# One layer of cross-attention, self-attention and a routed FFN: later waits and another PSUM bank where cross-attention hands over to self-attention

## The reference

```python
x = x + xattn(layernorm(x), ctx, mask, Wq, Wk, Wv, Wo)   # 16 heads of 32, 64 x 512 scores a sequence
x = x + attn(layernorm(x), wq, wk, wv, wo)               # rotary positions, causal, 64 x 64 scores
x = x + ffn(layernorm(x), w_router, W1, b1, W2, b2)      # half of each sequence's tokens, 512 -> 2048 -> 512
```

```python
# self-attention, the stage that begins where the change is
q, k, v = x @ wq, x @ wk, x @ wv
q, k = rope(q), rope(k)
scores = where(causal, q @ k.T / sqrt(32), -inf)
x = x + (softmax(scores) @ v) @ wo
```

## Time and profile before

| what | value |
|---|---|
| time, median of three executions | 1379.94 us (1377.67 to 1382.29) |
| time of the profiled execution | 1377.36 us |
| its span, first to last instruction | 1374.9 us |
| TensorE busy | 1341.6 us, 98% of the span |
| ScalarE, VectorE, GpSimd busy | 730.2, 666.7, 544.3 us |
| mean granted clock of TensorE | 0.995 of full speed |

### The profile page before, as it was taken

The page is one execution under the profiler, slowest core; times in us unless marked ns, Lnnn a source line. Parts: engine busy times, 40 slices in busy tenths (PEclk is TensorE's granted clock), DMA queues, the critical chain, the costliest instruction groups (busy, mean ns, idle before and its releaser), DMA issues.

```text
span 1374.9 us, 33152 instructions
## 1 busy us (share of the span) xinstructions
PE 1341.6 (98%) x12984; PEld 1059.8 (77%) x12984; DVE 666.7 (48%) x1688; ACT 730.2 (53%) x1410; POOL 544.3 (40%) x284
## 2 busy tenths in 40 slices
PE   7999999999999999999999999999999998999998
PEld 6877777777777777777777777677888886878686
DVE  4254554554544544544544544455666567732323
ACT  6455655656656656656656656653333345453231
POOL 6442422422522422422432434724444444466342
PEclk9999999999999999999999999999999999999999
DMA  7021111011011010110120112010000002122241
GB/s 254 26 59 34 34 50 32 28 54 32 25 57 32 25 57 26 31 57 25 32 57 25 32 56 93 14 55 2 1 0 0 0 0 93 62 92 92 77 138 61
DMA packets 39324, 66.06 MB, mean 48 GB/s; under 512 B 4208, under 2 KB 8560, under 8 KB 39280
## 3 DMA queue, kind: packets, MB, share of 16 engines
q1 hardware_dynamic: 38848, 64.67, 14.7%
q10 hardware_dynamic: 432, 0.79, 0.2%
HBM read 61.25 MB, written 4.19 MB: 48 GB/s over the span
## 4 chain that ended last, share of the span: by engine, by line
PE 89%; DVE 2%; ACT 2%; issue 1%; POOL 1%; POOLq 0%; DVEq 0%; ACTq 0%
PE psum L204 39%; PE psum L957 9%; PE psum L252 8%; PE psum L1791 6%; PE psum L1762 6%; PE psum L222 5%; PE psum L240 5%; PE psum L261 3%; PE psum L972 3%; PE psum L990 1%; PE psum L1448 1%; PE psum L982 1%; PE psum L1000 1%; PE psum L1773 1%; PE psum L1019 0%
## 5 line engine op out<-in xcount | busy, mean ns | idle before, releaser
L300 ACT ACTIVATE PT<-psum 128x512 f32<-128x512 f32 x256 | 153.2, 598 | 228.4 <-PE psum L252 228.4
L287 ACT ACTIVATE prob<-prob,nmx 128x512 f32<-128x512 f32 x256 | 182.6, 714 | 94.4 <-DVE nmx L342 94.4
L356 DVE COPY V<-psum 128x512 f32<-128x512 f32 x128 | 88.5, 692 | 229.4 <-PE psum L204 229.4
L342 DVE CUSTOM_DVE_ANT_0 prob<-psum,mbias 128x512 f32<-128x512 f32 x256 | 165.4, 684 | 67.1 <-PE psum L222 67.1
L293 ACT ACTIVATE prob<-prob,rinv 128x512 f32<-128x512 f32 x256 | 182.7, 714 | 0.0
L489 POOL TENSOR_SCALAR ctx_a<-ctx_r 128x1536 fp32r<-128x1536 f32 x16 | 65.4, 4090 | 265.3 <-PE psum L204 265.1
L489 POOL TENSOR_SCALAR ctx_b<-ctx_r 128x1536 fp32r<-128x1536 f32 x16 | 65.4, 4090 | 252.3 <-PE psum L204 235.4
L252 PEld LDWEIGHTS psum<-ident,prob 128*128 128x128 f32 x1024 | 127.5, 141 | 34.4 <-issue 1.3
L252 PE MATMUL psum<-ident,prob 128*128 128x128 f32 x1024 | 153.2, 272 | 0.5 <-ACT PT L300 0.4
L204 PE MATMUL psum<-wv_h,ctx_b 128*128 128x512 f32 x384 | 144.4, 417 | 0.0
L204 PE MATMUL psum<-wv_h,ctx_a 128*128 128x512 f32 x384 | 142.2, 412 | 1.2 <-DVE K L356 1.2
(11 more groups left out here) (215 smaller groups left out, 2814.2 us busy)
## 6 DMA issues: line engine op xcount, KB each, us to landing
ctx_r<-in_ctx SPq DMA_DIRECT2D x32, 768.0 KB, 4.6
w_r<-in_L_ffn_W SPq DMA_DIRECT2D x64, 256.0 KB, 2.8
xres<-in_x SPq DMA_DIRECT2D x16, 256.0 KB, 2.6
out<-tok SPq DMA_DIRECT2D x13, 256.0 KB, 3.6
tok<-in_x SPq DMA_DIRECT2D x3, 1024.0 KB, 12.4
mask<-in_mask_BxS_bf SPq DMA_DIRECT2D x32, 64.0 KB, 4.1
tok<-in_x SPq DMA_DIRECT2D x4, 256.0 KB, 3.3
wq_r<-in_L_xattn_Wq SPq DMA_DIRECT2D x4, 256.0 KB, 5.0
```

The costliest lines, as they stand in the source:

```text
L287: act.activation(prob[:, r, :], prob[:, r, :], ACT.Exp, bias=nmx[:, r:r + 1], scale=-1.0, accum_out=rsum[:, r:r + 1]).then_inc(s_ex, 1)
L300: act.activation(PT[:, r, :, :].rearrange("p k n -> p (k n)"), T_bank, ACT.Copy).then_inc(s_Pt, 1)
L342: dve.tensor_tensor_reduce(prob[:, r, :], S_bank[r], mbias[:, b, :], 1.0, 3.0e38, ALU.add, ALU.min, nmx[:, r:r + 1]).then_inc(s_mx, 1)
L356: dve.tensor_copy(item_place(q, m), KV_bank[m % 2]).then_inc(s_KVe, 1)
```

## The change

Three edits, all at the passage from cross- to self-attention.

1. TensorE's wait for `s3_xl` (tokens of tile 0 split into high and low parts) moves out of `first_tokens`, from ahead of item 1 to behind it, ahead of the first `pe_turn`, which is the next instruction that writes `T_bank`.
2. The transposed tokens of tiles 2 and 3 (steps 0 and 1) go to bank 2, no longer to bank 3, and TensorE waits for the rotation of Q (`s3_rq`), no longer for that of K (`s3_rk`), before it writes them.
3. The subtraction for `ow_l` on VectorE in step 1 moves from ahead of the rotation of K to behind `x3_l` of tile 3, ahead of the row sums.

```diff
@@ pe_group
             if fill:
                 fill()
             pe_item(pe, g, q, 1)
+            if filled:
+                pe.wait_ge(*filled)
             pe_turn(pe, g, q, 0, first)
@@ pe_cross
             def first_tokens():
                 pe.wait_ge(s_Pt, SLOTS - 8)
                 pe_x(pe, 0, T_bank)
-                pe.wait_ge(s3_xl, 1)
...
+                    if last and q == GPT - 2:
+                        pe_group(pe, g, q, first, fill=first_tokens, filled=(s3_xl, 1))
@@
+        def x_bank(t):
+
+            return bank[2] if isinstance(t, int) and t < 4 else bank[3]
@@ pe3
             if has(t + 2):
-                pe.wait_ge(s3_rk, 2 * t + 4)
-                pe_x(pe, t + 2, bank[3])
+                if isinstance(t, int) and t < 2:
+                    pe.wait_ge(s3_rq, 2 * t + 4)
+                else:
+                    pe.wait_ge(s3_rk, 2 * t + 4)
+                pe_x(pe, t + 2, x_bank(t + 2))
@@ act3, dve3
-                act_x(act, t + 2, par, bank[3])
+                act_x(act, t + 2, par, x_bank(t + 2))
...
-                dve_x(dve, t + 2, par, bank[3])
+                dve_x(dve, t + 2, par, x_bank(t + 2))
@@ dve3
             if isinstance(t, int) and t == 1:
                 shifts(dve, slice(G - 2, G), 2)
-                dve.wait_ge(s3_wa, 1)
-                dve.tensor_tensor(ow_l[:], ow_r[:], ow_h[:].bitcast(F32), ALU.subtract).then_inc(s3_wd, 1)
...
+            if isinstance(t, int) and t == 1:
+                dve.wait_ge(s3_wa, 1)
+                dve.tensor_tensor(ow_l[:], ow_r[:], ow_h[:].bitcast(F32), ALU.subtract).then_inc(s3_wd, 1)
             if has(t):
                 dve.wait_ge(s3_ex, t + 1)
```

More of the change, by code:

```diff
@@ L263, in pe_outputs, with pe_group @@
             ins.then_inc(s_Wo, 1)
-        def pe_group(pe, g, q, first=False, fill=None):
+        def pe_group(pe, g, q, first=False, fill=None, filled=None):
             pe_scores(pe, g, q, first)
@@ L795, in first_tokens @@
                 pe_x(pe, 0, T_bank)
-                pe.wait_ge(s3_xl, 1)
             def tile(g, first, last):
                 for q in range(GPT - 1 if last else GPT):
-                    pe_group(pe, g, q, first, fill=first_tokens if last and q == GPT - 2 else None)
+                    if last and q == GPT - 2:
+                        pe_group(pe, g, q, first, fill=first_tokens, filled=(s3_xl, 1))
+                    else:
+                        pe_group(pe, g, q, first)
             pe_item(pe, 0, -1, 2)
```

## The result

The changed kernel takes 1373.53 us (median of 6 runs, 1372.96 to 1374.11), the kernel before in the same comparison 1378.93 us (median of 6, 1377.67 to 1382.29). The ratio is 0.996, with a 95% interval of 0.9949 to 0.997: 0.4% faster. A second comparison gave 1373.81 against 1378.27 us, a ratio of 0.9965 (0.9951 to 0.9978). The forecast of 1376.0 us lies above both. Its range of 1373.2 to 1379.4 holds them, the first with 0.3 us to spare. In both the gain is over 0.3%, to which I had given a chance of 0.42; "within 0.3%" had 0.54.

What follows compares the result with a forecast made beforehand. TensorE, busy 98% of the span, was taken to bound the kernel. From 1379.94 us, 3.0 us (2.1 + 0.9) for the order of work and 0.9 us for the clock came off: 1376.0 us, range 1373.2 to 1379.4.

Steps and rivals of the forecast that it cites:

- Edit 1, 2.1 us: At tile 0, TensorE does item 1 before waiting for `x_l`: 2.1 us gained, bounds 1.5 and 2.15.
- Edit 2, nothing: Ahead of the token transposes of tiles 2 and 3, gaps of 0.50 and 0.61 us go, but nothing is gained.
- Edit 3, 0.9 us and not 2.1: At tile 2, `q_r` gets 2.1 us shorter, but K's last matmul limits the gain to 0.9 us, bounds 0 and 0.9.
- Where `ow_l` goes: Ahead of the row sums, `ow_l` waits for GpSimd's subtraction; the scaling still ends in time, with 2.3 us of slack.
- The gap at V stays: Ahead of V of tile 2, TensorE still waits some 2.2 us for `o_l`, only shifted.
- Sum 3.0 us: Whole passage: 2.1 us from the wait behind item 1 plus 0.9 us from moving `ow_l` later.
- The clock's 0.9 us: Removing the 2.15 us gap before `x_l` of tile 0 saves a 1.85 us clock fall, one chance in two: 0.9 us.
- B, the clock stays up at V of tile 2: Rival: no clock fall behind the gap at V of tile 2, 1.85 us more gained, 1374.2 us; chance 0.20.
- A: The forecast as computed for the whole kernel: 1376.0 us, own range 1374.2 to 1378.0; chance 0.52.
- C: Rival at tile 2: `q_r` is long because it directly follows the scaling, so moving `ow_l` gives nothing: 1376.9 us; chance 0.13.
- Case D: Rival in the stage behind the passage: more or longer clock falls give back 3.7 us, 1379.7 us; chance 0.10.
- E: Rival, slower: clock falls at the FFN's short waits; two more cost 3.7 us, four 7.4 us (1384.3); chance 0.05.

Runs made afterwards that it cites:

- changed, again: The changed kernel with all three edits, measured a second time beside the kernel before: 1373.81 us, ratio 0.9965.
- cut alone: The changed kernel with the subtraction for `ow_l` cut in three and its banks unchanged: 1374.27 us, ratio 0.9964 to the kernel before.

## Why the prediction was right, and where not

*Edit 1, 2.1 us*: right. 2.10 in the changed kernel's profile, and the same distance in edit 1 alone.

*Edit 2, nothing*: right, as far as it can be measured. Alone 0.9999, and the changed kernel without it is as fast.

*Edit 3, 0.9 us and not 2.1*: right. 0.89 in the profile, with K's last matmul as the new last wait.

*Where `ow_l` goes*: right. VectorE waits for GpSimd's subtraction. The scaling was forecast for 939.38 to 941.29, which with the 2.10 of edit 1 and the 0.79 of the start is 936.49 to 938.40; it runs from 936.27 to 938.18. The transposes that wait for it come at 939.14 and find it done, with 1.0 us to spare, less than the 2.3 of the forecast because the clock stayed up. By the Trainium skill (SBUF — State Buffer, "Who interferes with whom") the one that starts first keeps the port for its instruction; the trace agrees, 3.12 for 2.28 us here. In the version with `ow_l` in three, the half of it starts at 924.54 and takes its 1.21 us, and `q_r`, at 924.56, takes 2.34 us.

*The gap at V stays*: right, 2.11 us.

*Sum 3.0 us*: right for the order of work (2.10 + 0.89).

*The baseline*: 1.0 of the 2.5 us between forecast and result is not the change's. The forecast was counted from 1379.94 us, the median of three executions, and the kernel before stood at 1378.93 beside the changed one. The gain forecast was 3.9 us, measured were 5.4 and 4.5 us.

*The clock's 0.9 us*: the term that was wrong in its reason. The step was "the first gap, with one chance in two". Edit 1 alone, which removes that gap, shows no higher mean clock (0.9946). The changed kernel does: 0.9965 against 0.9945, which is 2 x 0.0020 x 1376 = 5.5 us less time at half clock. At most half of that, 2.8 us, is time won, and it will be less, because some of that time costs nothing: in the profile before, the granted clock is 0.50 from 1372.0 us to the end at 1374.9, and TensorE has no instruction there.

A better estimate comes from how the executions of one and the same kernel differ. Over 182 executions of all the kernels (each compared with the mean of its own kernel in its own comparison) 0.001 of mean clock goes with 0.6 us of span, so 0.0020 goes with about 1.2 us, an estimate that could be 0.6 us off either way. The mean span fell by 4.8 us, from 1376.4 to 1371.6: 3.0 by the order of work, about 1.2 with the clock, and some 0.6 that no run explains. The 0.35 us outside the span come on top. So 0.9 us was near the size of the clock's part, but by luck, since it was put at a gap that does not bring it.

How the higher clock comes about is not settled. The gap at V lowered the clock in 7 of the 9 profiles that have it, but only in two of the four whose order of work there is the changed kernel's (yes in changed, again, and without edit 2; no in changed and cut alone), and in none of the five in which the gap is filled or gone. That makes shorter and fewer gaps in the passage a likely cause, but each edit alone moved the mean clock by 0.0009 at most, about as much as before moved between comparisons (0.9939 to 0.9949), and there is one profile of each kernel, two of the changed one.

*B, the clock stays up at V of tile 2*: this rival, with 0.20 and 1374.2 us, is nearer to both medians than A. Its condition held in the changed kernel's first profile and not in the second, and in the first the low stretch that it saved came back at 1149. So neither A nor B describes every execution.

*C* is refuted: `q_r` directly behind the scaling takes 1.27 us. *Case D*, a longer low stretch later, is what the first profile shows at 1149 (twice 3.4 us); it came beside the gain and did not cancel it. *E* did not come: no fall behind the short waits of the FFN in the changed kernel's two profiles; the profile without edit 2 has one at 1273.6 us, 10.2 us long.

Of the signs that would have shown the prediction wrong none came: the chain still goes through `o_l` in step 1, TensorE does not wait for the scaling in step 2, and there are two low stretches before TensorE ends, for three.

## What to carry to other kernels

Put a wait at the instruction that overwrites, not at the one that happens to come next, and before counting on the length of a gap look at the chain: of three edits the one that removed two visible gaps gave nothing, since TensorE only waited for the next link. When an instruction that slowed a neighbour is moved away, the gain ends at the next last wait, here 0.9 of 2.1 us. The next edit is then the wait that TensorE still shows (`o_l`): another bank for what it guards, together with `ow_l` cut into idle times of VectorE so that the scaling is in time, gave 1.7 us more by the order of work and 3.7 in the median. Look at what the moved work meets at its new place.

## What the runs showed of the hardware that I had not expected

TensorE can stand without anything it waits for in the profile while a burst of DMAs lands, here eight loads of 256 KB for the FFN. It stood at one place between 1139 and 1147 us in all 13 profiles with the loads where they were: 0.1 to 0.2 us in before, each edit alone and the cut alone, 0.43 and 0.8 in the changed kernel, 0.5 without edit 2, 1.5 without edit 1, 1.3 in the two other kernels with new banks, 2.5 and 3.5 in the two with matmuls added ahead of it. In the one kernel where the loads were issued 6 us later it did not stand. Each time it went on 1.4 to 1.6 us after a 16 KB transfer on an instruction queue had ended, and in the one pair of kernels that differ only in the loads, that transfer came 3.0 us later with the loads in its way. From kernel to kernel the standstill differed by up to 3.3 us, more than an edit here is worth, and without edit 1 it was larger than before by more than the 0.9 us that edit 3 had won.

Adding matmuls to keep the clock up removed the low stretches behind the gaps that they filled, and made neither kernel faster beyond doubt: 0.9989 (0.9977 to 1.0) for the kernel before, and 1376.06 against 1373.81 us for the changed one, with a mean clock that stayed at 0.9965. And a gap of about 2 us lowers the clock in one execution and not in the next, with the same instructions at the same distance from each other: at 2.15 us in one of four profiles, at 2.1 to 3.0 us ahead of V in seven of nine.
